# ScalarE's softplus of the decay moved behind the copies of the keys' product

## The chip, the core and the metric

The kernel runs on one core of a Trainium2 chip. Time is device microseconds (us) for one whole execution. Before the change three runs took 3303.29 us in the median (3297.47 to 3306.33). One further execution was profiled, and every duration below is from that one.

## The reference, cut to what matters

A batch of 128 sequences of 32 tokens (512 channels) goes through cross-attention to 257 context rows, then a gated delta-rule attention (16 heads of 32 channels), then a mixture of eight experts. The change touches the second part:

```python
q = (x @ Wq.T).reshape(b, l, H, DH)
k = (x @ Wk.T).reshape(b, l, H, DH)
v = (x @ Wv.T).reshape(b, l, H, DH)
beta = jax.nn.sigmoid(x @ Wb.T).reshape(b, l, H, DH)
alpha = jnp.exp(-jnp.exp(A_log)[None, None, :] * jax.nn.softplus(x @ Wa.T + dt_bias))
q = q / jnp.linalg.norm(q, axis=-1, keepdims=True) / np.sqrt(DH)
k = k / jnp.linalg.norm(k, axis=-1, keepdims=True)
def step(S, inp):
    k_t, q_t, v_t, beta_t, a_t = inp
    S = S * a_t[..., None, None]
    kv_mem = jnp.einsum('bhd,bhde->bhe', k_t, S)
    delta = (v_t - kv_mem) * beta_t
    S = S + k_t[..., :, None] * delta[..., None, :]
    y_t = jnp.einsum('bhd,bhde->bhe', q_t, S)
    return (S, y_t)
```

## The kernel before, in words

**Units and passes.** The work is cut into 32 units of four sequences (128 rows, one per partition). The first pass (up to some 2600 us) does, in one turn per unit, the cross-attention of unit u and the second part's products of unit u-1. What is called unit n below is the n-th execution of the softplus, so it shares its turn with the cross-attention of the unit behind it. The second pass does the rest: outputs, routing, experts.

**Who does what in a turn.** TensorE writes most products into two PSUM banks used in turns (`ring`), in the order of the table `BOTH` in class `Ring`: the keys of the context (K00 to K23) mixed with products of the second part. The stretch that matters is K11, K12, the decay's product (`alpha_columns`, in `score`), KK (the keys' product), QQ (the queries'), K13, XT (a transpose), the product that sums the decays (L1024), K20, K21, the Gram matrices, BT, K22, K23, QT, V2 (L1050), and then the scores. A bank may be written again once ScalarE or VectorE has read it, so K13 waits until KK was copied and XT until QQ was. `move_kq` (L616 to L622) makes two passes over a product: a copy to `kq` and a square to `kq_squared`, both inside the tile `prob`; the square frees the bank.

**The decay.** VectorE waits for the decay's product and makes `minus_abs` (L764, L765). ScalarE's `softplus_log` makes its Exp and Ln (L626, L627). VectorE waits for that in `spread_decays` (L770 to L774), whose `steps_of` TensorE needs for L1024. VectorE's queue is in order: behind this wait stand steps of the delta rule, `read_grams` (L780 to L790, which waits for TensorE's Gram matrices), further steps, and the move of QT to `q_s` (L834). TensorE's last pair of V2 matmuls waits for `read_grams` and for that move.

**Delta-rule steps.** From unit 5 on VectorE carries, between these jobs, the 32 time steps of an earlier group of sequences (`time_step`, L169 to L176), spread over four units by the tables `STEPS` and `CUTS`. Step t works on t earlier rows, so it is longer for larger t. Units 5, 9, 13, ... carry steps 0 to 12, units 6, 10, 14, ... steps 13 to 20, units 7, 11, ... steps 21 to 26, and units 8, 12, ... steps 27 to 31; these are called first, second, third and fourth quarter. VectorE's program is a loop over groups of four units for units 5 to 28, while units 29 to 32 are written out with their own tables (`LAST_STEPS`, `LAST_CUTS`).

**GpSimd** multiplies the decay by a mask (L577), makes the norms (L579) and scales beta (L586) in the same stretch.

The order on every engine is the order in which the code is written; there is no scheduler.

Of the kernel before, what the change touches and what calls it, by code (L numbers as in the profile page):

```python
# [219 lines left out]
def first_pass(nc, ident, shared, early, x, cond_t, cond_last_t, q_w, q_b, kv_w, kv_b, proj_w, proj_b, attn_w_t, wa_t,  # L220
               dt_bias, a_log, norm_w, v_last_d, rows):
    with ExitStack() as ctx:
# [381 lines left out]
        @block.scalar  # L604
        def _(act):
            own = Own(act, act_steps)

            def move(name, u, dst, func=ACT.Copy, **how):
                bank = ring.wait_full(act, name, u)
                act.activation(dst, ring_bank[bank][:], func, **how).then_inc(ring.free[bank], 1)  # L610

            def move_keys(u, piece, group):
                bank = ring.wait_full(act, f"K{piece}{group}", u)
                at, n = PIECES[piece]
                act.activation(k_t[:, group, at:at + n], ring_bank[bank][:, 0:n], ACT.Identity,  # L615
                               bias=kvb[:, group:group + 1]).then_inc(ring.free[bank], 1)  # L616

            def move_kq(u, i, name):
                bank = ring.wait_full(act, name, u)
                act.activation(kq[:, :, i * N:i * N + N], ring_bank[bank][:].rearrange("p (g t) -> p g t", t=N),  # L620
                               ACT.Copy)
                act.activation(kq_squared[:, i], ring_bank[bank][:], ACT.Square).then_inc(ring.free[bank], 1)  # L622

            def softplus_log(u):
                act.wait_ge(minus_abs_ready, u)
                own.then(act.activation(minus_abs[:], minus_abs[:], ACT.Exp))  # L626
                act.activation(log_part[:], minus_abs[:], ACT.Ln, bias=1.0).then_inc(log_ready, 1)  # L627

            def wait_stored(stored, u, each=16):
                if not (isinstance(u, int) and u == 1):  # L630
                    act.wait_ge(stored, (u - 1) * each)

            def sigmoid_begun(name, u, dst, copy=None):

                bank = ring.wait_full(act, name, u)
                if copy is not None:
                    act.activation(copy, ring_bank[bank][:], ACT.Copy)
                ins = act.activation(dst, ring_bank[bank][:], ACT.Exp, scale=-1.0)
                ins.then_inc(ring.free[bank], 1)

            def sigmoid_ended(name, u, dst):
                ring.wait_read(act, name, u)
                own.then(act.activation(dst, dst, ACT.Ln, bias=1.0))
                return act.activation(dst, dst, ACT.Exp, scale=-1.0)  # L644

            def exponentials(u, b):
                act.wait_ge(neg_max_ready, u * BU + b + 1)
                for g in range(HG):
                    act.activation(prob[:, b % 2, g, :], score[:, g, 0:M], ACT.Exp, bias=neg_max[:, g:g + 1],  # L649
                                   accum_out=sums[:, g:g + 1]).then_inc(exp_done, 1)  # L650

            def move_turned(u, b):
                act.wait_ge(turned_ready, u * BU + b + 1)
                act.activation(prob_t[:, 0, :], turned[0][:], ACT.Copy).then_inc(prob_t0_ready, 1)

            def high_terms(u, b):
                act.wait_ge(cond_loaded[b % 2], (u * 2 + b // 2) * 16 + 16)
                cols = slice(b * M, (b + 1) * M)
                act.activation(cond_high[:, :, cols], cond[:, b % 2], ACT.Copy).then_inc(high_done, 1)

            def move_attended(u, b):
                bank = ring.wait_full(act, f"O{b}", u)
                for a in range(HG):
                    last = act.activation(att_t[:, a, b * N:b * N + N], ring_bank[bank][:, a * N:a * N + N], ACT.Identity,
                                          bias=kvb[:, HG + a:HG + a + 1])
                last.then_inc(ring.free[bank], 1)

            def turn(u, first=False, last=False, more=True):
                a, b_ = not last, not first
                if a:  # L670
                    for g in range(4):
                        move_keys(u, 0, g)
                    move_keys(u, 1, 0)
                if b_:
                    move("X1T", u, x1n_t[:].rearrange("p c t -> p (c t)"))
                if a:
                    move_keys(u, 1, 1)
                    move_keys(u, 1, 2)
                if b_:
                    softplus_log(u)  # L680
                    move_kq(u, 0, "KK")
                    move_kq(u, 1, "QQ")
                if a:
                    move_keys(u, 1, 3)
                    move("XT", u, xn_t[:].rearrange("p c t -> p (c t)"))
                if b_:
                    wait_stored(qk_stored, u)
                    act.wait_ge(sums_ready, u)
                    act.activation(decay[:].rearrange("p h t -> p (h t)"), turned[0][:], ACT.Exp).then_inc(decay_ready, 1)
                if a:  # L690
                    move_keys(u, 2, 0)
                    move_keys(u, 2, 1)
                if b_:
                    wait_stored(pairs_stored, u, 48)
                    sigmoid_begun("BT", u, vgb[:, 2, :])
                    sigmoid_ended("BT", u, vgb[:, 2, :]).then_inc(beta_ready, 1)
                if a:
                    move_keys(u, 2, 2)
                    move_keys(u, 2, 3)
                if b_:  # L700
                    move("V2", u, vgb[:, 0, :])
                if a:
                    for b in range(BU):
                        exponentials(u, b)
                        if b > 0:
                            move_turned(u, b - 1)
                        move(f"V{b}0", u, v_s[:, b % 2, 0, :])
                        move(f"V{b}1", u, v_s[:, b % 2, 1, :])
                        if more:
                            high_terms(u + 1, b)  # L710
                        if b > 0:
                            move_attended(u, b - 1)
                    move_turned(u, BU - 1)
                silu = steps_of[:].rearrange("p h t -> p (h t)")
                if a:
                    move_attended(u, BU - 1)
                if b_:
                    wait_stored(gate_stored, u)
                    sigmoid_begun("GT", u, silu, copy=vgb[:, 1, :])
                    sigmoid_ended("GT", u, silu).then_inc(silu_ready, 1)  # L720

            act.preload_act_table_set("natural_log_exp_and_others")
            per_turn = 3
            for b in range(BU):
                high_terms(0, b)
            turn(0, first=True)
            turn(1)
            with act.Fori(2, NU - 1) as u:
                own.turn(per_turn, u - 2, per_turn)
                turn(u)  # L730
                assert own.n == per_turn
            own.turn((NU - 2) * per_turn, 0, 0)
            turn(NU - 1, more=False)
            turn(NU, last=True)
# [994 lines left out]
```

## Time and profile before

| | us |
|---|---|
| median of three runs | 3303.29 (3297.47 to 3306.33) |
| the profiled execution: its time | 3298.92 |
| its span | 3296.9 |
| TensorE matmul busy | 3106.4 (94%) |
| VectorE busy | 2007.4 (61%) |
| ScalarE busy | 1336.0 (41%) |
| GpSimd busy | 642.1 (19%) |
| mean granted TensorE clock, share of full | 0.969 |

Busy time is a sum over the whole span. TensorE is nearly always busy, so a change tells where it makes TensorE wait, or ends such a wait. The other engines have idle time in sum, but each works its queue in order, and a turn repeats about every 80 us.

### The profile page before, as it was taken

How to read it: one execution, taken by the hardware profiler on the slowest of the kernel's cores; microseconds unless marked ns; L12 is line 12 of the kernel's file. 1: busy time of each engine (PE TensorE's matmuls, PEld its weight loads, DVE VectorE, ACT ScalarE, POOL GpSimd, SP SyncE). 2: the span in 40 equal slices, each digit the busy share in tenths (PEclk: the TensorE clock that was granted, in tenths of full speed). 3: DMA queues.
4: the chain of work that ended last, by engine and by line, in shares of the span. 5: the costliest groups of instructions: out<-in, count | busy, mean ns of one | idle time of the engine just before them, and what ended most of it. 6: DMA issues, size and time to landing. Idle time of an engine off the chain costs nothing. (4 is left out here: it accounts for less than half of the span.)

```text
span 3296.9 us, 87695 instructions
## 1 busy us (share of the span) xinstructions
PE 3106.4 (94%) x35570; PEld 2274.9 (69%) x35570; DVE 2007.4 (61%) x4107; ACT 1336.0 (41%) x3360; POOL 642.1 (19%) x514
## 2 busy tenths in 40 slices
PE   6999999999999999999999999999999788898995
PEld 5777777777777777777777777777777555544542
DVE  3333366756766677567666675766676487893323
ACT  3444444444444444444444444444443233322321
POOL 0011111111111111111111111111111276601334
PEclk9999999999999999999999999999999898899997
DMA  4222322232223222222222222222321688535479
GB/s 167 69 73 86 102 95 80 88 101 84 81 79 97 84 80 80 97 89 80 79 97 84 84 84 97 84 81 79 101 85 64 148 252 258 175 131 164 136 265 329
DMA packets 297853, 378.10 MB, mean 115 GB/s; under 512 B 159568, under 2 KB 211536, under 8 KB 296016
## 3 DMA queue, kind: packets, MB, share of 16 engines
q1 hardware_dynamic: 287184, 338.19, 32.3%
q0 software_dynamic: 10240, 33.56, 2.9%
q8 instruction: 346, 5.67, 0.7%
q14 instruction: 83, 0.68, 0.1%
HBM read 258.17 MB, written 189.01 MB: 136 GB/s over the span
## 5 line engine op out<-in xcount | busy, mean ns | idle before, releaser
L120 PE MATMUL ring<-cond_high,wkv_high 128*128 128x342 f32 (+1 forms) x1152 | 406.0, 352 | 57.0 <-issue 20.0
L120 PE MATMUL ring<-cond_low,wkv_high 128*128 128x342 f32 (+1 forms) x1152 | 373.2, 324 | 0.0
L120 PE MATMUL ring<-cond_high,wkv_low 128*128 128x342 f32 (+1 forms) x1152 | 371.9, 323 | 0.0
L615 ACT ACTIVATE shared_rows<-ring,kvb 128x342 f32<-128x342 f32 (+1 forms) x384 | 209.4, 545 | 381.4 <-PE ring L120 381.4
L840 DVE TENSOR_REDUCE neg_max<-score 128x4 f32<-128x1028 f32 x128 | 157.3, 1229 | 289.0 <-PE score L947 289.0
L120 PE MATMUL ring<-wkv_high,cond_high 128*128 128x512 f32 x768 | 316.6, 412 | 0.0
L169 DVE TENSOR_TENSOR prod<-coef,deltas 128x64 f32<-128x64 f32 (+30 forms) x248 | 308.7, 1245 | 5.9
L120 PE MATMUL ring<-wkv_high,cond_low 128*128 128x512 f32 x768 | 303.0, 395 | 0.0
L120 PE MATMUL ring<-wkv_low,cond_high 128*128 128x512 f32 x768 | 302.8, 394 | 0.0
L120 PEld LDWEIGHTS ring<-cond_high,wkv_high 128*128 128x128 f32 x1152 | 220.4, 191 | 107.6 <-issue 54.7
L649 ACT ACTIVATE prob<-score,neg_max 128x257 f32<-128x257 f32 x512 | 235.9, 474 | 135.6 <-DVE neg_max L840 135.6
L120 PE MATMUL mix<-experts,xs_t 128*128 x624 | 287.2, 604 | 0.0
L173 DVE TENSOR_TENSOR prod<-prod 128x256 f32<-128x256 f32 (+5 forms) x352 | 258.2, 734 | 12.1
L120 PE MATMUL ring<-wattn,x1n_t 128*128 128x512 f32 x512 | 248.4, 619 | 0.3 <-ACT prob L622 0.3
L569 POOL TENSOR_TENSOR vgb<-vgb,steps_of 128x512 f32<-128x512 f32 x32 | 40.4, 1263 | 1067.4 <-ACT steps_of L644 1067.4
L120 PE MATMUL ring<-x1n_t,wattn 128*128 128x128 f32 x2048 | 239.3, 278 | 0.0
L120 PEld LDWEIGHTS ring<-x1n_t,wattn 128*128 128x128 f32 x2048 | 234.1, 194 | 0.0
L120 PEld LDWEIGHTS ring<-cond_low,wkv_high 128*128 128x128 f32 x1152 | 219.8, 191 | 15.4 <-issue 15.4
L120 PEld LDWEIGHTS ring<-cond_high,wkv_low 128*128 128x128 f32 x1152 | 220.1, 191 | 0.0
L610 ACT ACTIVATE v_s<-ring 128x512 f32<-128x512 f32 x256 | 154.0, 602 | 158.5 <-PE ring L120 158.5
L120 PEld LDWEIGHTS mix<-experts,xs_t 128*128 128x128 f32 x624 | 115.1, 194 | 116.7 <-issue 116.7
L120 PEld LDWEIGHTS ring<-wkv_high,cond_high 128*128 128x128 f32 x768 | 144.5, 188 | 63.0 <-issue 34.8
(199 smaller groups left out, 5502.9 us busy)
## 6 DMA issues: line engine op xcount, KB each, us to landing
cond<-cond_t_dram SPq DMA_DIRECT2D x128, 385.5 KB, 4.2
xs<-slot_rows SPq DMA_DIRECT2D x78, 256.0 KB, 2.8
slot_rows<-ys SPq DMA_DIRECT2D x78, 256.0 KB, 2.0
x_rows<-x SPq DMA_DIRECT2D x64, 256.0 KB, 2.7
vb_rows<-vgb SPq DMA_DIRECT2D x64, 256.0 KB, 3.5
x_in<-x_dram SPq DMA_DIRECT2D x32, 256.0 KB, 3.2
kk_rows<-kk_rows_s SPq DMA_DIRECT2D x32, 256.0 KB, 2.7
qk_rows<-decay SPq DMA_DIRECT2D x32, 256.0 KB, 2.8
```

The source lines that it names most:

```text
L120: last = pe.matmul(out, lhs_t, rhs, start=start and i == 0, stop=stop and i == len(terms) - 1)
L169: own.then(dve.tensor_tensor(tiles["prod"][:, 0:t], coef, tiles["deltas"][:, 0:t], ALU.mult))
L173: own.then(dve.tensor_tensor(tiles["prod"][:, 0:half], tiles["prod"][:, 0:half], tiles["prod"][:, left:whole], ALU.add))
L569: own.then(pool.tensor_tensor(vgb[:, 1], vgb[:, 1], steps_of[:].rearrange("p h t -> p (h t)"), ALU.mult))
L610: act.activation(dst, ring_bank[bank][:], func, **how).then_inc(ring.free[bank], 1)
L615: act.activation(k_t[:, group, at:at + n], ring_bank[bank][:, 0:n], ACT.Identity, bias=kvb[:, group:group + 1]).then_inc(ring.free[bank], 1)
L649: act.activation(prob[:, b % 2, g, :], score[:, g, 0:M], ACT.Exp, bias=neg_max[:, g:g + 1], accum_out=sums[:, g:g + 1]).then_inc(exp_done, 1)
L840: dve.tensor_reduce(neg_max[:], score[:, :, 0:M], AX.X, ALU.max, negate=True)\
```

## The change

In `turn` of ScalarE's program, `softplus_log(u)` stands between the two `move_kq` calls and no longer ahead of them. No instruction is added or removed, and the other engines' programs are the same.

```diff
@@ -677,8 +677,8 @@
                     move_keys(u, 1, 1)
                     move_keys(u, 1, 2)
                 if b_:
+                    move_kq(u, 0, "KK")
                     softplus_log(u)
-                    move_kq(u, 0, "KK")
                     move_kq(u, 1, "QQ")
                 if a:
                     move_keys(u, 1, 3)
```

ScalarE's queue in the loop over the units, at the copies of KK and QQ (`prob` is the tile that holds both copies and squares; `shared_rows` holds the context's keys; L80 and L100 are register instructions of the loop):

```order
 L615 ACTIVATE shared_rows<-ring,kvb 128x342 [waits ring1_full]
+L80 REGISTER_ALU
+L620 ACTIVATE prob<-ring 128x16x32 [waits ring0_full]
+L622 ACTIVATE prob<-ring 128x512
 L626 ACTIVATE minus_abs<-minus_abs 128x16 [waits minus_abs_ready]
 L100 ISA
 L627 ACTIVATE log_part<-minus_abs 128x16 [waits scalar_steps]
-L80 REGISTER_ALU
-L620 ACTIVATE prob<-ring 128x16x32 [waits ring0_full]
-L622 ACTIVATE prob<-ring 128x512
 L620 ACTIVATE prob<-ring 128x16x32 [waits ring1_full]
 L622 ACTIVATE prob<-ring 128x512
```

Exp and Ln, with their wait for VectorE, now stand behind the wait for TensorE's KK, and the copy of KK no longer stands behind the wait for VectorE.

The same place in the units that are written out ahead of the loop:

```order
 L615 ACTIVATE shared_rows<-ring,kvb 128x342 [waits ring1_full]
+L620 ACTIVATE prob<-ring 128x16x32 [waits ring0_full]
+L622 ACTIVATE prob<-ring 128x512
 L626 ACTIVATE minus_abs<-minus_abs 128x16 [waits minus_abs_ready]
 L627 ACTIVATE log_part<-minus_abs 128x16 [waits scalar_steps]
-L620 ACTIVATE prob<-ring 128x16x32 [waits ring0_full]
-L622 ACTIVATE prob<-ring 128x512
 L620 ACTIVATE prob<-ring 128x16x32 [waits ring1_full]
 L622 ACTIVATE prob<-ring 128x512
```

It is the same exchange; the last unit, which has no context keys in front, has it too.

## Rows read from the trace of the kernel before

**Rows 1.** Waits: engine, line, waited for: us in total, times, longest.
```profile
PE ring L120 <- ACT prob L622: 15.8, 7, 3.5
PE ring L1050 <- DVE q_s L834: 6.0, 2, 3.3
DVE x L873 <- PE turned L120: 213.2, 32, 7.5
DVE square L780 <- PE score L996: 79.5, 15, 13.9
```
**Rows 2.** Timeline, ScalarE, unit 13: start, length, what, idle before.
```profile
1065.44 0.21 ACT L626 ACTIVATE minus_abs<-minus_abs 128x16 f32<-128x16 f32 x1 [8.19 <-DVE minus_abs L765]
...
1066.29 0.59 ACT L622 ACTIVATE prob<-ring 128x512 f32<-128x512 f32 x1
...
1067.24 0.61 ACT L622 ACTIVATE prob<-ring 128x512 f32<-128x512 f32 x1
```
**Rows 3.** Timeline, TensorE, unit 13: KK and QQ, K13, L1024.
```profile
1057.32 7.39 PE L120 MATMUL ring<-x1n_t,wattn 128*128 128x128 f32 x64
1066.93 0.50 PE L120 MATMUL ring<-cond_high,wkv_high 128*128 128x342 f32 x1 [2.23 <-ACT prob L622]
...
1070.36 1.12 PE L1024 MATMUL turned<-steps_of,later 128*128 128x512 f32 x2
```
**Rows 4.** Windows: busy of PE, PEld, DVE, ACT, POOL; granted clock; DMA.
```profile
1067.13:1070.55 3.41, 3.41 (x14) 3.35 (x14) 3.24 (x7) 1.27 (x3) 0.00 (x0) 0.50 0.00 0
```
**Rows 5.** Timeline, unit 13, later: TensorE's V2, VectorE's Gram read and QT move.
```profile
1087.26 3.60 PE L1050 MATMUL ring<-wattn,x1n_t 128*128 128x512 f32 x8
...
1077.51 0.17 DVE L780 COPY square<-score 128x16 f32<-128x16 f32 x1 [1.12 <-PE score L996]
...
1087.65 0.69 DVE L834 SCALAR_TENSOR_TENSOR q_s<-ring,qb_scaled 128x512 f32<-128x512 f32 x1
```
**Rows 6.** Timeline, unit 14 (second quarter): TensorE, ScalarE, VectorE.
```profile
1139.82 7.39 PE L120 MATMUL ring<-x1n_t,wattn 128*128 128x128 f32 x64
...
1165.71 3.66 PE L1050 MATMUL ring<-wattn,x1n_t 128*128 128x512 f32 x8
...
1143.71 0.22 ACT L626 ACTIVATE minus_abs<-minus_abs 128x16 f32<-128x16 f32 x1 [3.96 <-DVE minus_abs L765]
...
1167.43 0.69 DVE L834 SCALAR_TENSOR_TENSOR q_s<-ring,qb_scaled 128x512 f32<-128x512 f32 x1
```
**Rows 7.** Timeline, unit 14: two equal VectorE pairs, and GpSimd.
```profile
1146.49 1.15 DVE L173 TENSOR_TENSOR prod<-prod 128x512 f32<-128x512 f32 x2
...
1150.18 2.13 DVE L173 TENSOR_TENSOR prod<-prod 128x512 f32<-128x512 f32 x2
...
1150.74 1.29 POOL L577 TENSOR_TENSOR decay<-decay,up_to 128x512 f32<-128x512 f32 x1 [17.24 <-ACT decay L689]
```
**Rows 8.** Timeline, unit 15 (third quarter): ScalarE, TensorE, VectorE.
```profile
1221.14 0.21 ACT L626 ACTIVATE minus_abs<-minus_abs 128x16 f32<-128x16 f32 x1 [2.94 <-DVE minus_abs L765]
...
1222.12 0.60 ACT L620 ACTIVATE prob<-ring 128x512 f32<-128x512 f32 x1 [0.51 <-PE ring L120]
...
1227.39 1.02 PE L1024 MATMUL turned<-steps_of,later 128*128 128x512 f32 x2
...
1244.16 3.60 PE L1050 MATMUL ring<-wattn,x1n_t 128*128 128x512 f32 x8
...
1245.43 0.69 DVE L834 SCALAR_TENSOR_TENSOR q_s<-ring,qb_scaled 128x512 f32<-128x512 f32 x1
```
**Rows 9.** Timeline, unit 16 (fourth quarter): VectorE's move of QT.
```profile
1324.32 0.69 DVE L834 SCALAR_TENSOR_TENSOR q_s<-ring,qb_scaled 128x512 f32<-128x512 f32 x1 [1.35 <-PE ring L120]
```
**Rows 10.** Timeline, unit 30 (second quarter, written out): ScalarE and TensorE.
```profile
2424.83 0.22 ACT L626 ACTIVATE minus_abs<-minus_abs 128x16 f32<-128x16 f32 x1 [2.28 <-DVE minus_abs L765]
...
2426.47 0.60 ACT L620 ACTIVATE prob<-ring 128x512 f32<-128x512 f32 x1 [1.17 <-PE ring L120]
...
2454.58 1.10 PE L1050 MATMUL ring<-wattn,x1n_t 128*128 128x512 f32 x2 [3.33 <-DVE q_s L834]
```

## The prediction, made before the changed kernel ran

> **What bounds the kernel now.** I read the busy shares first: TensorE is at 94%, so only what moves TensorE moves the end. Next come the waits, for what TensorE waits for at this place [rows 1]. It waited seven times for the square of KK (L622), 15.8 us in all and 3.5 at most, and twice for VectorE's move of QT (L834), 6.0 us. So the present order does cost something, and the other engine at this place, VectorE, has already touched TensorE from the other side. The same view says how far a disturbance carries: VectorE waits for TensorE at L873 in all 32 turns (213.2 us in 32 times) [rows 1]. At the end of a turn VectorE always catches up, so every turn can be reckoned alone and the turns added. Then I read the timelines of a group of four, units 13 to 16, and of unit 30.
>
> **What is removed: the wait for KK's copy.** In unit 13 VectorE is late: ScalarE stood 8.19 us before the softplus could start at 1065.44 [rows 2]. TensorE's KK and QQ are equal halves of 7.39 us, so KK was full at 1061.1, and its copy stood ready to go for over 4 us. TensorE ended QQ and idled 2.23 us until the square of KK freed the bank [rows 3]. After it the granted clock fell to 0.50 of full (1.2 for 2.4 GHz) for 3.41 us [rows 4], which costs about half of it, 1.7 us, of which 1.2 fall ahead of L1024. After the change KK is copied at once and K13 goes on without a wait. What is late next is QQ: its copies stand behind the softplus. Between the two squares lie 0.95 us [rows 2], the pair of KK that is now done earlier, so QQ's square starts at 66.29 in place of 67.24 and ends at 1066.9. XT can start then, and L1024 0.6 us later, near 1067.5 in place of 1070.36 [rows 3]: 2.9 us earlier.
>
> Not all of that stays. TensorE's last pair of V2 takes 1.1 us [rows 10] of the 3.6 [rows 5], so here it began 2.5 us into V2, at 1089.8. VectorE finished QT at 1088.34 [rows 5], 1.4 earlier. VectorE's own start of the turn does not move; only its 1.12 us wait for the Gram matrices [rows 5] goes, so QT can be done at 1087.2 at the earliest. V2's last pair starts at 1087.4, a gain of 2.4, and I take 2.2, since GpSimd's work now falls elsewhere in VectorE's queue. There are five such units, 9, 13, 17, 21 and 25: 5 x 2.2 = **11 us gained**. The two left of the seven are units 31 and 32. In unit 31 VectorE holds V2 up later in the turn anyway (the second wait of L1050 in rows 1), and in unit 32 the copies of QQ, not of KK, are what is waited for. I count nothing for them.
>
> **What is added: a wait of VectorE.** Where VectorE is early, its `spread_decays` now waits for KK and its two copies. A copy and a square start 0.48 us apart (half of 0.95), so the Exp starts 1.0 us after KK is full. Queued behind it on VectorE are steps, the Gram read, steps, and the move of QT; TensorE's last pair of V2 waits for that.
>
> Units 1 to 4 carry no steps: VectorE idles up to 13.9 us before the Gram read [rows 1], and a delay of a third of that is hidden there. So it is for L1024: in unit 15 `steps_of` would be ready 1.7 us after an Exp at 1223.1, at 1224.8, and L1024 starts at 1227.39 [rows 8].
>
> Second quarter (units 6, 10, 14, 18, 22, 26). In unit 14 KK is full at 1139.82 + 3.8 = 1143.6, so the Exp starts at 1144.6 and not at 1143.71: VectorE is 0.9 us later. It has nothing to spare: QT was done at 1168.12, and the last pair of V2 started at 1165.71 + 3.66 - 1.10 = 1168.3 [rows 6, 10]. To this comes GpSimd. The same pair of additions took 1.15 us alone and 2.13 where GpSimd's L577 began inside it [rows 7]: up to 1.0 us per meeting. L577 and L586 keep their place behind TensorE, while VectorE slides under them. Laying the steps 0.9 us later against these two, I find that unit 14 keeps its first meeting and gets a second of 0.7 us, with L586. So 0.9 + 0.7 = 1.6 us. Since the Exp now hangs on KK in all six units, they become alike, whatever their old slack: 6 x 1.6 = **9.6 us lost**.
>
> The Trainium skill, page "SBUF — State Buffer", section "Who interferes with whom", speaks against the change here: a VectorE instruction with two inputs in SBUF and a GpSimd instruction that reads SBUF exclude each other for the whole instruction. By that rule, the trace agrees with 0.98 us on an addition of this kind. Without it the sum of this part would be some 5 us smaller.
>
> Third quarter (7, 11, 15, 19, 23, 27). In unit 15 KK was full at 1222.1 (its copy started at once, 1222.12), so the Exp would start at 1223.08, not 1221.14: 1.94 later [rows 8]. The last pair of V2 started at 1244.16 + 2.5 = 1246.7, and QT was done at 1246.12: 0.5 to spare. Both meetings with GpSimd stay about what they are. 6 x 1.45 = **8.7 us lost**.
>
> Fourth quarter. The delay is like unit 15's, under 2 us. But in unit 16 VectorE waits 1.35 us for TensorE's QT, and has moved it at 1325.0 [rows 9]; V2 starts when QT is full and its last pair comes 2.5 us later, at 1326.8, so there are 1.35 + 1.8 us to spare. Nothing is lost.
>
> Last group. In unit 30 VectorE already holds TensorE up by 3.33 us. The Exp goes from 2424.83 to 2427.43 [rows 10], 2.6 later, nearly all of it straight onto TensorE: **2.4 us lost**, and 0.4 in unit 31 by a new meeting with GpSimd. The idle there grows to 5.7 us; a fall of the clock like that of rows 4 may follow, which I count at 1.5.
>
> ScalarE's other work hides the rest: it stands idle ahead of these copies in every unit shown [rows 2, 8].
>
> **The sum.** Lost 9.6 + 8.7 + 2.4 + 0.4 = 21.1, gained 11, clock 1.5: net +11.6. The profiled execution took 3298.9 (span 3296.9 and 2.0 around it), so 3310.5 after. That execution was 4.4 us under the median of the runs, 3303.3, which with the same step becomes 3314.9. I say 3314.
>
> Bounds. The gain is at most what TensorE gets earlier in unit 13, 2.9 us, in five units: 14.5. At least it is nothing, if VectorE were late by another 2.4. The loss per unit of the second and third quarter lies between the delay less the slack with no new meeting (0.9 and 1.45) and that with a whole further meeting of 1.0 (1.9 and 2.4). That makes the loss 14.1 to 25.8 + 2.8, so the net goes from about +2.5 to +28. I take the values laid out, which lie nearest to the rows of units 14 and 15.
>
> **The rivals.**
> The meetings with GpSimd do not get worse. Then the second quarter loses 0.9 in most units, and less where it had slack; the net is about +6: 3309. For it: some units of this quarter have lost nearly as much to GpSimd as they could. Against: VectorE slides into L577 and L586, not away.
>
> VectorE catches up before V2, and only the gain stays. It decides in the steps between the Exp and the QT move: if units 14 and 15 had over 2 us of idle there, all of the delay would be swallowed. That gives -11: 3292, faster. For it: VectorE is busy only 61% and waits 15 times at the Gram read [rows 1]. Against: in units 14 and 15 the move of QT starts with no idle before it [rows 6, 8], and the idle is in units 1 to 5 and the fourth quarter.
>
> The clock. If each new idle of 1.5 us lowers the clock as the 2.23 us one did, twelve more falls of up to 1.5 us come: +18 more, 3332. Against: the new idles are a third shorter than that one.
>
> The softplus doesn't hold KK's copy back at all. That would give no gain and the loss alone, +22: 3325. Against it stands the row in which the copies follow the Exp within 1 us after 8.19 us of waiting.
>
> **How the numbers follow.** Main forecast 0.52, meetings no worse 0.22, only the gain 0.08, clock 0.08, no gain 0.04, and 0.06 for gain and loss cancelling near 3303. A difference under 0.3%, 9.9 us, cannot be told from none for this kernel. The main case, +11.6, lies just above that line: with a few us of doubt I give it 0.7 of being slower by over 0.3% and the rest within. With clock and no gain, and a tenth of the second case, slower has 0.50; faster has 0.07; within has 0.43. The main case alone is 3309 to 3320. The range, 3300 to 3326, takes in the second case and leaves out the gain-only and clock cases.
>
> **What would show it.** Right: TensorE no longer waits for L622 at K13; VectorE waits for L627 by 1 to 4 us in most units; TensorE waits for L834 in about twelve more units, 1.4 to 1.7 us each, and near 5.8 us in unit 30; the clock no longer falls right behind QQ in units 9 to 25. Wrong: no waits of TensorE for L834 in units 10, 14, 15, or a fall of the clock in most of them.

## The result, and the profile after

| | before | after |
|---|---|---|
| median of 10 runs each, us | 3302.11 (3297.47 to 3326.41) | 3313.56 (3309.55 to 3323.54) |
| ratio to before | | 1.0036, 95% interval 1.0022 to 1.0051 |
| profiled execution's span, us | 3296.9 | 3308.1 |

It was timed twice more, on other occasions and beside the kernel before: 1.0073 (1.0057 to 1.0090) and 1.0048 (1.0033 to 1.0064). It is slower in all three, by 11.5, 24.5 and 16.4 us in the medians. The first two intervals don't overlap, so the size is less certain than the direction; f1 and g1 below come back to it.

The waits in the profile after, from 95 us on (engine, line, waited for: us in total, times, longest). They answer to [rows 1]:

```profile
DVE log_decay L770 <- ACT log_part L627: 78.2, 32, 4.8
...
DVE square L780 <- PE score L996: 41.2, 5, 9.7
...
PE ring L1050 <- DVE q_s L834: 27.7, 17, 5.6
...
PE ring L927 <- ACT prob L622: 10.5, 5, 3.1
```

TensorE's wait for the square of KK at K13 is gone, and a smaller one (L927, 10.5 us in place of 15.8) stands a little later, at XT, for the square of QQ. Its wait for VectorE's move of QT went from 2 times and 6.0 us to 17 times and 27.7. VectorE waits for the softplus 78.2 us in all, and for the Gram matrices 5 times in place of 15: where it idled at the Gram read before, it now idles one job earlier.

Unit 17, of the first quarter, ScalarE and then TensorE (start, length, what, idle before). It answers to [rows 2, 3] of unit 13:

```profile
1382.22 0.60 ACT L620 ACTIVATE prob<-ring 128x512 f32<-128x512 f32 x1 [3.92 <-PE ring L120]
...
1387.12 0.22 ACT L626 ACTIVATE minus_abs<-minus_abs 128x16 f32<-128x16 f32 x1 [3.81 <-DVE minus_abs L765]
1387.37 0.22 ACT L627 ACTIVATE log_part<-minus_abs 128x16 f32<-128x16 f32 x1
1387.49 0.58 ACT L620 ACTIVATE prob<-ring 128x512 f32<-128x512 f32 x1
```
```profile
1385.51 0.40 PE L120 MATMUL ring<-cond_high,wkv_high 128*128 128x342 f32 x1
...
1388.70 0.63 PE L927 MATMUL ring<-ident,x_in 128*128 128x128 f32 x4 [1.51 <-ACT prob L622]
1389.17 1.02 PE L1024 MATMUL turned<-steps_of,later 128*128 128x512 f32 x2
```

KK is copied as soon as it is full, K13 starts with no idle, and the softplus holds only QQ back, so XT waits 1.51 us. Two windows follow (busy of PE, PEld, DVE, ACT, POOL; granted clock; DMA). The first is at the place in unit 17 where the clock had fallen in the first-quarter units, and now it is at 1.00. The second is in unit 30, together with TensorE's last pair of V2 there:

```profile
1387.99:1391.40 3.41, 2.70 (x15) 2.25 (x16) 3.12 (x8) 2.20 (x5) 0.43 (x1) 1.00 0.02 5
...
2458.40:2465.20 6.80, 4.89 (x38) 2.27 (x39) 2.88 (x5) 0.91 (x2) 1.05 (x1) 0.50 0.03 6
```
```profile
2460.31 2.04 PE L1050 MATMUL ring<-wattn,x1n_t 128*128 128x512 f32 x2 [5.65 <-DVE q_s L834]
```

Unit 14, of the second quarter: ScalarE, VectorE, GpSimd, TensorE. It answers to [rows 6, 7]:

```profile
1141.48 0.60 ACT L620 ACTIVATE prob<-ring 128x512 f32<-128x512 f32 x1 [3.92 <-PE ring L120]
1141.97 0.59 ACT L622 ACTIVATE prob<-ring 128x512 f32<-128x512 f32 x1
1142.45 0.22 ACT L626 ACTIVATE minus_abs<-minus_abs 128x16 f32<-128x16 f32 x1
```
```profile
1142.95 0.17 DVE L770 SCALAR_TENSOR_TENSOR log_decay<-z,log_part 128x16 f32<-128x16 f32 x1 [3.10 <-ACT log_part L627]
...
1148.89 2.13 DVE L173 TENSOR_TENSOR prod<-prod 128x512 f32<-128x512 f32 x2
...
1159.27 2.01 DVE L173 TENSOR_TENSOR prod<-prod 128x576 f32<-128x576 f32 x2
...
1166.84 0.69 DVE L834 SCALAR_TENSOR_TENSOR q_s<-ring,qb_scaled 128x512 f32<-128x512 f32 x1
```
```profile
1148.55 1.47 POOL L577 TENSOR_TENSOR decay<-decay,up_to 128x512 f32<-128x512 f32 x1 [18.83 <-ACT decay L689]
...
1159.35 1.58 POOL L586 TENSOR_TENSOR vgb<-vgb,inv_square 128x512 f32<-128x512 f32 x1
```
```profile
1163.53 2.74 PE L1050 MATMUL ring<-wattn,x1n_t 128*128 128x512 f32 x6
1167.68 1.10 PE L1050 MATMUL ring<-wattn,x1n_t 128*128 128x512 f32 x2 [1.41 <-DVE q_s L834]
```

The Exp starts 1.0 us after KK is full, VectorE waited 3.10 us for it, and V2's last pair starts 4.15 us into V2, where it was 2.56 before: 1.6 us lost. The two pairs of additions meet L577 (2.13 us, as before) and L586 (2.01 us). The same second pair took 1.29 us in the kernel before:

```profile
1160.57 1.29 DVE L173 TENSOR_TENSOR prod<-prod 128x576 f32<-128x576 f32 x2
```

The six units of this quarter in the loop wait 1.41 or 1.42 us each, the six of the third 1.44.

Unit 15, of the third quarter. It answers to [rows 8]; the last line, by itself, is the same multiplication in the kernel before:

```profile
1222.77 0.22 ACT L626 ACTIVATE minus_abs<-minus_abs 128x16 f32<-128x16 f32 x1
...
1228.92 2.85 DVE L169 TENSOR_TENSOR prod<-coef,deltas 128x1536 f32<-128x1536 f32 x1
...
1248.03 1.10 PE L1050 MATMUL ring<-wattn,x1n_t 128*128 128x512 f32 x2 [1.44 <-DVE q_s L834]
```
```profile
1227.31 1.76 DVE L169 TENSOR_TENSOR prod<-coef,deltas 128x1536 f32<-128x1536 f32 x1
```

### The profile page after: what moved, and what is told of

It is laid out like the page before. It is cut to its first block and busy times, and to the rows that moved or that the text cites. A ratio compares the mean times of both kernels' runs of the same rounds, so it can differ in the third digit from the quotient of the medians.

```text
span 3308.1 us, 87695 instructions
## 1 busy us (share of the span) xinstructions
PE 3096.1 (94%) x35570; PEld 2264.6 (68%) x35570; DVE 2011.3 (61%) x4107; ACT 1334.0 (40%) x3360; POOL 639.0 (19%) x514
## 3 DMA queue, kind: packets, MB, share of 16 engines
q8 instruction: 345, 5.65, 0.7%
```

## The experiments

The kernel before was timed again beside each group. The four e kernels were timed together, the four f kernels together on another chip, and the three g kernels together at a third time. The ratio is not always the ratio of the two medians to the last digit; the interval belongs to the ratio.

| kernel | median us | before | ratio | 95% interval |
|---|---|---|---|---|
| e1_first_quarter_only | 3297.18 | 3302.32 | 0.9975 | 0.9958 to 0.9992 |
| e2_unrolled_old_order | 3302.95 | 3302.32 | 0.9999 | 0.9983 to 1.0015 |
| e3_step_ahead_of_decay | 3297.31 | 3302.32 | 0.9976 | 0.9959 to 0.9992 |
| e4_softplus_behind_both | 3409.71 | 3302.32 | 1.0313 | 1.0279 to 1.0347 |
| f1_changed_again | 3327.64 | 3303.12 | 1.0073 | 1.0057 to 1.0090 |
| f2_beta_behind_v2 | 3309.55 | 3303.12 | 1.0020 | 1.0001 to 1.0038 |
| f3_all_but_first_quarter | 3334.71 | 3303.12 | 1.0104 | 1.0087 to 1.0120 |
| f4_step_ahead_and_beta | 3291.28 | 3303.12 | 0.9952 | 0.9935 to 0.9969 |
| g1_changed_third | 3315.74 | 3299.35 | 1.0048 | 1.0033 to 1.0064 |
| g2_beta_alone | 3294.55 | 3299.35 | 0.9990 | 0.9972 to 1.0008 |
| g3_best_again | 3283.96 | 3299.35 | 0.9963 | 0.9950 to 0.9977 |

**e1: the gain alone.** The edit is against the changed kernel; `...` marks what is left out.

```diff
-                    move_kq(u, 0, "KK")
+                    keys_first = quarter == 0
+                    if keys_first:
+                        move_kq(u, 0, "KK")
                     softplus_log(u)
+                    if not keys_first:
+                        move_kq(u, 0, "KK")
                     move_kq(u, 1, "QQ")
...
-            with act.Fori(2, NU - 1) as u:
...
+            with act.Fori(0, NG - 2) as group:
+                own.turn(before, group, GU * per_turn)
+                for quarter in range(GU):
+                    turn(group * GU + (LAG + quarter), quarter=quarter)
```

> Only units of the first quarter (1, 5, 9, ... 29) copy KK ahead of the softplus, all others keep the old order; for that ScalarE's loop body holds four units in place of one. Theory (the cost is VectorE's later softplus in the second and third quarter, the gain is KK's early copy in the first): the gain alone stays, about -11 us against the kernel before (3291 against 3302), TensorE waits for VectorE's move of QT (L834) only by some 0.8 us in units 9 to 25, and in units 30 and 31 as before; no wait at K13 in units 9, 13, 17, 21, 25. Rival (the gain is an accident of the clock falls, and the exchange costs in any unit): no more than 3 us from the kernel before.

Measured -0.25%, some 8 us (5 in the medians), less than the 11 forecast. The interval, 3 to 14 us, doesn't reach zero, but it doesn't exclude the rival's 3 us for certain. What decides against the rival is the waits. They are, for the same stretch, in e1:

```profile
DVE log_decay L778 <- ACT log_part L627: 28.9, 32, 4.8
...
PE ring L1058 <- DVE q_s L842: 9.4, 7, 3.4
PE ring L935 <- ACT prob L622: 8.6, 5, 2.4
```

(The lines behind ScalarE's program lie 8 further on here.) The wait at K13 is gone. For the move of QT TensorE waits in no unit of the second or third quarter of the loop; of the 9.4 us, 6.0 are those of units 30 and 31, as before the change. So the exchange pays where VectorE is late.

**e2: the longer loop body alone.** As e1, with `keys_first = False`: the old order in every unit.

> The old order in every unit, with ScalarE's loop body of four units as in e1: what the longer body itself costs. Theory: nothing, within 3 us of the kernel before, since ScalarE idles over half of each turn. Rival (fetching a longer body holds ScalarE up at each way back): some us slower, which would have to be taken off e1.

Ratio 0.9999 (0.9983 to 1.0015). e1's gain isn't owed to the longer loop body.

**e3: fill VectorE's wait.** Against the changed kernel, on VectorE. What is left out lets `some_steps` carry only a part of its steps.

```diff
...
+                lead = 1 if quarter in (1, 2) else 0
                 if not first:
                     log_decays(u)
+                    some_steps(1, end=lead)
                     spread_decays(u)
-                some_steps(1)
+                some_steps(1, start=lead)
```

> The changed order of ScalarE, and on VectorE, in units of the second and third quarter, one delta-rule step (3.6 or 4.6 us of work) stands between minus_abs and the wait for the softplus. Theory (the loss is VectorE's idle there): VectorE waits for L627 only in the first and fourth quarter, TensorE's waits for L834 of 1.4 us in the 12 units go, in unit 30 it falls from 5.6 to about 3.3 us, and the gain stays: about -11 us against the kernel before. Rival (GpSimd's meetings carry the loss, not the idle): waits of 0.7 us or more stay in these units, and the time is within 4 us of the kernel before. Second rival: the step makes the sum of the decays late (L1024 waits for steps_of), some 1 us in each third-quarter unit.

Measured -0.24% (0.9959 to 0.9992), again less than the 11 us forecast, with ScalarE's order that of the changed kernel. VectorE in unit 14, and the waits:

```profile
1142.01 0.23 DVE L175 TENSOR_TENSOR rec<-vb_steps,rec 128x64 f32<-128x64 f32 x1
1142.27 0.23 DVE L176 TENSOR_TENSOR deltas<-rec,vb_steps 128x64 f32<-128x64 f32 x1
1142.53 0.17 DVE L770 SCALAR_TENSOR_TENSOR log_decay<-z,log_part 128x16 f32<-128x16 f32 x1
```
```profile
PE ring L1053 <- DVE q_s L837: 6.3, 5, 3.3
PE turned L1027 <- DVE steps_of L774: 2.8, 1, 2.8
```

One step ahead of the wait and L770 follows with no idle; all waits of TensorE at V2 in the second and third quarter of the loop are gone (5 are left: 0.75 in four first-quarter units, 3.31 in unit 30). The time alone wouldn't exclude the first rival, whose 4 us lie within the interval; the absent waits do. The second rival came true in one place only: unit 31, where VectorE is late already, makes L1024 wait 2.81 us.

**e4: a larger dose.** Both `move_kq` calls stand ahead of `softplus_log(u)`.

> The softplus stands behind the copies of KK and of QQ, 3.6 us later than in the changed kernel: a larger dose. Theory: VectorE's move of QT is late by another 3.6 us, so TensorE waits at V2 about 5 us in each of the 12 units of the second and third quarter, 2.4 in the 6 of the fourth, 2.5 in units 5 and 29, 11 in unit 30, and L1024 waits about 1 us in the units without steps; lost about 93, gained 11, so +80 us against the kernel before (3382). Rival (the slack elsewhere takes it up, or the loss in the changed kernel is GpSimd's meetings, which do not grow with the delay): at most +20 us.

Measured +107 us in four runs, where 80 was forecast; the rival's 20 is out. The waits:

```profile
DVE log_decay L770 <- ACT log_part L627: 178.2, 31, 8.3
PE ring L1050 <- DVE q_s L834: 69.2, 27, 7.5
PE turned L1024 <- DVE steps_of L774: 26.1, 31, 1.4
```

TensorE waits at V2 for 3.3 us in the second quarter and 3.8 in the third, less than the 5 I gave. L1024 now waits 0.77 us in most units, which moves the TensorE work behind it by as much. The two rows make 95 us against 6.0 in the kernel before [rows 1]. The clock makes up most of the rest. TensorE's idle time of all causes, from the first unit's KK to the last unit's V2, grew by 83 us (52 to 135). The time at a granted clock of 0.50 in the same stretch grew from 41 to 92 us, and half of that growth, 26 us, is what it costs. Together that is 109 of the 113 us by which the stretch grew. V2's last pair shows such a fall, at 2.05 us where it is else 1.10:

```profile
1210.77 2.05 PE L1050 MATMUL ring<-wattn,x1n_t 128*128 128x512 f32 x2 [3.31 <-DVE q_s L834]
```

That is the clock rival of the prediction, at a dose over twice as large: a fall lies at 9 of the 11 V2 waits of 3.3 to 3.8 us. At the 1.4 us waits of the changed kernel no fall followed, in none of 47 such waits in the profiles of after, f1, g1 and f3.

**f1 and g1: the changed kernel again.**

> The changed kernel once more, beside the next three on one chip. Theory: +10 to +12 us against the kernel before (ratio 1.003 to 1.0035), with TensorE's waits for L834 of 1.4 us in 12 units as in its first profile.

> The changed kernel a third time, since its second timing came out at +0.73% and its first at +0.36%. Theory: its waits account for some +11 us, so this one is +0.3 to +0.4% again, and the runs spread by chip and execution. Rival (the change costs more than the profile shows): +0.7% again.

The first expectation is missed: +0.73%. The second gave +0.48%, between the two. The profiled executions are not typical of their groups: f1's took 3305.1 us, the fastest of its six (median 3327.6), and g1's took 3329.7, the slowest of its nine (median 3315.7). So no trace shows what made the median of f1. The two profiles can be compared with each other. Their spans were 3303.1 and 3327.7 us, with the same waits for VectorE and a different idle time of TensorE that ended with no release by another engine ("issue"), at the beginning of turns:

```profile
PE ring L1050 <- DVE q_s L834: 29.7, 18, 5.7
PE ring L120 <- issue: 15.2, 20, 2.0
```
```profile
PE ring L1050 <- DVE q_s L834: 30.1, 19, 5.6
PE ring L120 <- issue: 29.2, 23, 2.1
```

The first fence is f1, the second g1. A stop of 1.5 to 2.1 us ahead of the first keys of a turn came in 15 turns of g1 and in 6 of f1 (9 in the profile of before, 7 in the first of after). It makes up 14 of the 25 us between those two executions. Another 4 us lie in the part behind the first pass, which the change doesn't touch. Whether the change makes these stops more frequent in the runs without a profile is open: no run here tells it apart.

**f2: GpSimd's part.** Against the changed kernel, on GpSimd.

```diff
+                ring.wait_read(pool, "V2", u)
                 pool.wait_ge(beta_ready, u)
                 pool.wait_ge(squares_ready, 2 * u)
                 pool.tensor_tensor(by_head(2), by_head(2), each_channel(inv_square[:]), ALU.mult).then_inc(vb_ready, 1)
-                ring.wait_read(pool, "V2", u)
```

> The changed kernel, with GpSimd's scaling of beta (L586) moved behind the copy of V2, past VectorE's move of QT. Theory (the meeting with L586 is 0.73 us of each unit's wait at V2): those waits fall from 1.41 to 0.68 us in the second quarter and from 1.44 to 0.71 in the third, from 0.76 to nearly nothing in the first; in all about 11 us less than the changed kernel, so level with the kernel before. Rival (VectorE's idle alone makes the wait, GpSimd's part is hidden): waits and time as in the changed kernel.

TensorE's last pair of V2 in unit 10, and the waits:

```profile
844.84 1.10 PE L1050 MATMUL ring<-wattn,x1n_t 128*128 128x512 f32 x2 [0.69 <-DVE q_s L834]
```
```profile
PE ring L1050 <- DVE q_s L834: 13.9, 12, 4.9
```

The wait fell from 1.41 to 0.69 us as stated, and in all from 29.7 (f1, the same chip) to 13.9. The time fell by half a per cent against f1, 18 us where 11 was forecast, and it stayed 6 us above the kernel before, where it should have been level. The waits account for 16 us. The rival, "waits and time as in the changed kernel", is out by the waits; the time alone is less sure, since f2's interval (1.0001 to 1.0038) is clear of f1's but overlaps those of the changed kernel's other two timings. The meeting is real and about half of the loss in these units.

**f3: the loss alone.** As e1, with `keys_first = quarter != 0`.

> The new order in all units but those of the first quarter, which keep the old one (ScalarE's loop body of four units, as in e1 and e2). Theory (the loss without the gain): waits of 1.4 us at V2 in 12 units and 5.6 in unit 30, and the waits at K13 of 2 to 3 us with their clock falls are all still there: about +20 us against the kernel before (3322). Rival (loss and gain are tied together): about +11 us, as the changed kernel.

+31.6 us, where 20 was forecast. Both waits stand side by side:

```profile
PE ring L1058 <- DVE q_s L842: 25.7, 15, 5.6
...
PE ring L120 <- ACT prob L622: 15.6, 6, 3.9
```

Loss and gain come apart, and the changed kernel lies between e1 and f3. f1 and f3 came out some 13 and 12 us over their theory, f2 beside them 6, and f4 at most 5. So the excess was larger where more of the waits at V2 were left. That may mean that the exchange costs more in executions that weren't profiled than these waits show; it isn't tested, and it belongs to what was left open above.

**f4 and g3: the version that beats both.** e3 without the early step in unit 31, and f2's order on GpSimd.

```diff
+                written_out = isinstance(group, int)
+                lead = 1 if quarter == 1 or (quarter == 2 and not written_out) else 0
```

> e3 (one step ahead of the wait for the softplus in the second and third quarter) without that step in unit 31, where it made L1024 wait 2.8 us, and with L586 behind V2 as in f2. Theory: the gains add, no wait of TensorE for L834 over 0.3 us but in units 30 and 31, -13 to -17 us against the kernel before (3287), the fastest here. Rival (beta's scaling now meets VectorE in the softmax part and delays that): as e3 or slower, 3297 or more.

> f4 once more. Theory: -12 to -16 us against the kernel before (ratio 0.995 to 0.9965).

-0.48% and -0.37%: some 12 to 16 us under the kernel before, with both intervals clear of 1. In g3 TensorE waits for VectorE's move of QT by more than 0.1 us only in units 30 and 31:

```profile
PE ring L1054 <- DVE q_s L838: 4.5, 2, 2.5
```

How much of this the move of L586 gives beyond e3 isn't shown: the intervals of e3, f4 and g3 overlap.

**g2: f2's order on the kernel before.**

> The kernel before, with only GpSimd's scaling of beta behind the copy of V2. Theory (with the old order VectorE moves QT in time in the 12 units, so what GpSimd takes from it is slack): within 3 us of the kernel before; only units 30 and 31 may wait 0.7 us less. Rival (the meeting costs the kernel by itself, whatever the order): -9 us, as much as it gave in f2.

0.9990 (0.9972 to 1.0008): no difference that can be told. With the old order what GpSimd takes from VectorE is slack outside units 30 and 31. There the waits fell from 3.33 to 2.85 us and from 2.67 to 1.95.

## Why the prediction was right

The time of the first ten runs, 3313.56, stands 0.4 us from the 3314 stated, and 11.5 us over the kernel before, where 11.6 was forecast. The direction and the mechanism are as forecast; that the number came so near is partly luck. The two later timings give 24.5 and 16.4 us, and 3327.6 would lie just outside of the stated range. And the terms miss in both directions. How long TensorE takes from the start of KK to V2's last pair can be read for every unit (28.5 us in the undisturbed ones). The differences between the profiles of before and after are these; the clock of unit 30 is reckoned apart, since the fall lies mostly behind that pair:

| | forecast, us | in the profile of after, us |
|---|---|---|
| second quarter, six units | 9.6 lost | 9.5 lost |
| third quarter, six units | 8.7 lost | 9.6 lost |
| first quarter, five units | 11 gained | 7.3 gained |
| unit 30 | 2.4 lost, and 1.5 for the clock | 2.3 lost, and up to 3.4 for the clock |
| units 31 and 32 | 0.4 lost | 3.2 gained |

Unit 5 was 1.7 us faster, because a fall of the clock in the profile of before was absent. In all, the stretch from the first unit's KK to the last unit's V2 took 8.4 us longer (2503.4 to 2511.8). The part behind it, which the change doesn't touch, took 4.2 us longer, which is spread (692.6 to 704.5 us over all profiles here), and the part ahead of it 1.4 less. Together these make the 11.2 us between the two spans. Step by step:

- **Gain, 5 x 2.2.** The mechanism is as stated: K13 no longer waits, XT waits for QQ, and VectorE becomes the limit at V2 (0.76 us in units 9, 17 and 21). From KK full to V2's last pair unit 17 went from 29.4 to 27.25 us, 2.1 gained. In f1, where VectorE reached `minus_abs` about as early as before, or earlier, in all five units, they gained 1.9, 1.7, 2.5, 4.9 and 2.6, or 13.6. In the profile after, units 13 and 25 gained nothing. VectorE itself reached `minus_abs` 2.2 and 1.3 us later after the start of KK in those turns; XT then waited 3.1 and 2.8 us and the clock fell once each. Most of the delay is in an idle of VectorE that no other engine's release ends and that comes once in each group of four units: 6.25 and 6.30 us ahead of L744 in these two, 4.56 and 4.76 in the same units before. That spread was not in the prediction, which held that VectorE's own start doesn't move. e1 gives 8 us for the whole gain, with an interval of 3 to 14. Unit 13, the profile of after and then that of before:

```profile
1053.98 0.15 DVE L744 TENSOR_SCALAR var_eps<-mean_var 128x1 f32<-128x1 f32 x1 [6.25 <-issue]
```
```profile
1056.35 0.15 DVE L744 TENSOR_SCALAR var_eps<-mean_var 128x1 f32<-128x1 f32 x1 [4.56 <-issue]
```

- **Second quarter, 6 x 1.6.** 1.6 measured, with the second meeting of VectorE and GpSimd at the named instruction and of the named size (0.72, forecast 0.7); f2 took it away and got it back.
- **Third quarter, 6 x 1.45.** 1.6 measured. "Both meetings stay about what they are" held in number, and not quite in size: the meeting with L577 fell on a longer operation, 2.85 us in place of 1.76, and so cost 1.09 us where it had cost 0.97.
- **Fourth quarter and units 1 to 4, nothing.** Right: no wait of TensorE there. In e4, at 3.6 us more, the fourth quarter waits 1.5.
- **Unit 30, 2.4 and the clock.** The wait grew from 3.33 to 5.65 us, and the clock was at 0.50 for 6.8 us there, which costs half of it, over twice the 1.5 us counted. Not all of that is owed to the change: e3's 3.31 us wait in this unit had 6.8 us at 0.50 too, and e1's 3.36 us had 3.4. That the profile of before showed none here was chance. In unit 31 the wait stayed 2.66 in the first profile and was 4.5 in f1 and g1; the new meeting of 0.4 us that the prediction counted there is not confirmed.
- **The rivals.** "Only the gain" fell with the twelve waits and with f3. "No gain" fell with e1. "Meetings no worse" fell with the second meeting in unit 14 and with f2. The clock rival was false at 1.4 us and true at the dose of e4.

What was weak is the claim of a single number for the sum. The profiled executions of the changed kernel alone differ by up to 25 us, over half of it in stops that have nothing to do with the waits reckoned here.

## What to carry to other kernels

An instruction that waits should stand behind work that is ready and ahead of work that isn't; which of two this is can differ from turn to turn, so read all phases of the schedule, and find the queue whose next job decides. A wait moved to another engine costs the part that exceeds that engine's slack, and an idle that was harmless at one place (15 waits at the Gram read) does not cover the same idle one job earlier. Where a wait can't be avoided, put a piece of independent work of its length ahead of it, as e3 did with one step.

## What the runs showed of the hardware

- VectorE additions and multiplications with both inputs in SBUF were longer where a GpSimd multiplication (L577 or L586) overlapped them: by 0.72 us (2.01 for 1.29), 0.98 (2.13 for 1.15) and 1.09 (2.85 for 1.76). L586 itself took 1.58 us in unit 14 of the profile after, and 1.05 at the least. In units 14 and 15, sliding VectorE's queue by 1 or 2 us kept the meeting with L577, once on another instruction, and in unit 14 added one with L586.
- In the first pass of the kernel before, TensorE's granted clock fell to 0.50 within 2 us of the end of 7 of its 8 idles of 2.2 to 3.5 us, and of 2 of its 9 stops of 1.5 to 1.9 us. After waits of 1.36 to 1.45 us at V2 it fell in none of 47.
- Executions of the changed kernel differ by stops of TensorE of 1.5 to 2.1 us at the beginning of turns, 6 to 15 of them, that no other engine's release ends. Over all profiles here it is 6 to 15 of 31 turns. VectorE has stops of the same kind once per group of four units, 2.5 to 3.0 us and then 4.5 to 6.3 us in before, after and f1. What makes them isn't shown.
